# Cross attention's softmax tiles and context as fp16 pairs transposed by DMA, gate products on VectorE, in a decoder layer kernel

## The chip, the cores and the metric

One core of one Trainium2 chip runs the whole program. The metric is device time in microseconds (us); for a kernel on one core that is the time of this core. The kernel before took 362.12 us, the median of 3 runs (362.05 to 362.48).

## The reference

One decoder layer on x of 8 batches x 512 tokens x 256 features, in fp32, with a context of the same shape:

```python
x = x + _L0_attn_ref(_layernorm(x), head_dim_mask, w_q, w_k, w_v, w_o)
x = x + _L0_xattn_ref(_layernorm(x), ctx, mask, W, b)
x = x + _L0_ffn_ref(_layernorm(x), w_gate, w_up, w_down)

# _L0_attn_ref: q, k, v = x @ w_q, x @ w_k, x @ w_v        (256 -> 128)
#   y = (softmax(q k^T / sqrt(128)) v * head_dim_mask) @ w_o
# _L0_xattn_ref: x_proj = relu(x W^T + b); y_proj = relu(ctx W^T + b)   (256 -> 256)
#   scores = x_proj y_proj^T, -inf where the mask is set; y = softmax(scores) ctx
# _L0_ffn_ref: bitlinear(x, w) = _act_quant(x) @ _weight_quant(w)^T
#   gate = silu(bitlinear(x, w_gate)); up = bitlinear(x, w_up)          (256 -> 1024)
#   y = bitlinear(gate * up, w_down)                                    (1024 -> 256)
#   _act_quant: a row is scaled to 127 over its maximum and rounded
#   _weight_quant: mean of |w| is the scale, values rounded to -1, 0, 1
```

## The kernel before

A batch n (0 to 7) is one unit: 512 tokens, as T = 4 tiles of 128 tokens on the partitions, 256 features as DC = 2 chunks of 128. The work is written as steps of four streams: A is self attention, B cross attention, C the feed-forward part, E the projection of the context; W and F prepare weights, and S names the DMA transfers of a batch. Five lists written out by hand (PE_ORDER, ACT_ORDER, DVE_ORDER, POOL_ORDER and SP_ORDER, L102 to L250) give the order of the steps on TensorE (PE), ScalarE (ACT), VectorE (DVE), GpSimd (POOL) and on the DMA queue of SyncE (SP). Each engine runs its list in order, and every step waits on semaphores for its inputs and for the buffers that it overwrites. Three or four batches are in work at once: at a given time A is at batch n+3, B at n+2 and C at n or n+1.

fp32 precision comes from pairs: a value is split into a rounded high part and a rest, hi + lo, and a product is three matmuls, hi x hi, lo x hi and hi x lo (`product3`, L1133 to L1137, which all products by pairs share, so that their rows differ by tile names). The usual split of a result in PSUM is one ScalarE copy that rounds (hi) and one VectorE subtraction (lo).

Stream A: norms on VectorE and GpSimd (power of -0.5, L745), projections Q, K, V, four score steps S0 to S3, exponential on ScalarE (L931). For batches n > 0 the exponential of a tile goes to PSUM (the bank of its S step), ScalarE rounds it to fp16 (`p16`, L888) and VectorE subtracts for the rest (L1539); a DMA transposes the pair of the tile (`p16T`, L604), and the H step multiplies it by the fp16 pair of V.

Stream E, B: the transposed context (`ctxT_raw`) is loaded, rounded on ScalarE (`round_ctxT`) and its rest taken on GpSimd (`ctxT_rest`); W is split in the same way (`wt_hi`, `wt_lo`). YP0 and YP1 are the projection of the context, with relu (`yp_relu`) and a rest on GpSimd. XT0 and XT1 transpose the normed x on TensorE, their results are split (L941, L1594), XP0 and XP1 project. A tile t of cross attention then is: S_t, the scores (six matmuls of 512 columns: two chunks by three products); VectorE adds the mask and takes the maximum into `b_p` and `b_nmax` (L1600); ScalarE's exponential with the sum (L961); P_t, four TensorE transposes of `b_p` into a PSUM bank (L1280); ScalarE rounds them (`b_pT_hi`, L939), VectorE takes the rest (`b_pT_lo`, L1594); O_t, twelve matmuls of 256 columns by the context (`ctx_hi` from `round_ctx` on ScalarE, L975, and `ctx_lo` from `ctx_rest` on GpSimd, L689), and VectorE adds the result, scaled, to x (L1605). `b_p` and `b_pT` have two slots; the B steps alternate between the two banks b0 and b1.

Stream C: x is quantised (bf16), transposed by DMA (`xqT`), and for each tile pair j of 0 to 7 there is a gate product g_j and an up product u_j (L1352). ScalarE takes tanh of the gate (L1023); VectorE multiplies (t + 1) by g (L1624). For n < 6 ScalarE copies the up product out of PSUM (L1026) and GpSimd multiplies the two (`gated`, L753); for n = 6 and 7 VectorE multiplies them directly from PSUM (L1619). Then h is quantised over its row maximum (L1651, L800), copied to bf16 by ScalarE (L1033), transposed by DMA (`hT`, L612), and multiplied by the down weights (L1372).

## Time and profile before

| | value |
|---|---|
| device time, median of 3 runs | 362.12 us (362.05 to 362.48) |
| span of the profiled execution | 359.9 us |
| TensorE matmul busy | 349.1 us (97%) |
| TensorE weight load busy | 258.2 us (72%), beside matmuls |
| VectorE busy | 312.9 us (87%) |
| ScalarE busy | 313.7 us (87%) |
| GpSimd busy | 293.1 us (81%) |
| time of the packets of the DMA queue | 50.3% of 16 engines' span |

The span is one execution taken by the hardware profiler, from its first to its last instruction; 2.2 us lie between it and the median of the runs. Busy shares are means over a start of about 82 us without gate products and the rest with them. TensorE's instructions are pipelined, so the durations of neighbours overlap; the distance between their starts is what one costs. A row of the timeline gives start, duration, engine, line, operation, output <- input, shape and count; a group row gives busy time and mean ns of one, and then the idle time of the engine just before, with what ended most of it.

### The profile page before, as it was taken

What the parts mean: (1) busy time and instruction counts of PE and PEld (TensorE: products, weight loads), DVE (VectorE), ACT (ScalarE), POOL (GpSimd) and SP (SyncE); (2) the same over time, 40 slices, a digit from 0 to 9 for tenths busy, and PEclk for the clock granted to TensorE, in tenths of its full rate; (3) what the DMA queues carried; (4) which work ended last, traced back from release to release, by engine and by line L of the source; (5) the groups of instructions that cost most, each with busy time, mean ns of one, the idle gap of its engine ahead of it and who ended that gap; (6) DMA issues with size and microseconds to landing.
All of it is one profiled execution on the core that took longest, in us unless ns stands there. A gap on an engine that the chain in (4) does not pass through costs nothing.

```text
span 359.9 us, 7050 instructions
## 1 busy us (share of the span) xinstructions
PE 349.1 (97%) x1922; PEld 258.2 (72%) x1948; DVE 312.9 (87%) x916; ACT 313.7 (87%) x583; POOL 293.1 (81%) x421
## 2 busy tenths in 40 slices
PE   8999899999999999999999999999899999999996
PEld 6476578876887767776786678777587768667655
DVE  3769949948899899998899889999899889899994
ACT  2598999999899977999889986999679988987995
POOL 1657779369899998899968998899877997895886
PEclk9999999999999999999999999999999999999999
DMA  7986731725206644557275568238434633312353
GB/s 264 425 229 221 189 90 31 140 67 197 54 14 139 143 146 122 103 124 172 92 176 120 112 180 240 47 81 170 90 58 94 157 55 79 73 32 44 61 163 131
DMA packets 84695, 46.09 MB, mean 128 GB/s; under 512 B 76208, under 2 KB 77872, under 8 KB 84272
## 3 DMA queue, kind: packets, MB, share of 16 engines
q1 hardware_dynamic: 84656, 45.64, 50.3%
q8 instruction: 16, 0.26, 0.3%
q14 instruction: 23, 0.19, 0.2%
HBM read 23.07 MB, written 4.21 MB: 76 GB/s over the span
## 4 chain that ended last, share of the span: by engine, by line
PE 71%; DVE 8%; ACT 8%; POOL 5%; issue 5%; DMA 1%; SPq 1%; ACTq 0%; DVEq 0%; POOLq 0%
PE b_bank L1135 7%; PE b_bank L1136 7%; PE b_bank L1137 7%; PE d_bank L1372 5%; PE g_bank L1352 5%; PE a_bank L1135 5%; PE u_bank L1352 5%; PE a_bank L1137 5%; PE a_bank L1136 5%; PE b_bank L1280 2%; PE a_bank L1217 2%; POOL xp_lo L706 2%; PE b_bank L1251 1%; PE e_bank L1135 1%; PE e_bank L1137 1%
## 5 line engine op out<-in xcount | busy, mean ns | idle before, releaser
L753 POOL TENSOR_TENSOR c_work<-c_work 128x512 f32<-128x512 f32 x48 | 61.4, 1290 | 6.5 <-DVE c_work L1624 4.6
L1023 ACT ACTIVATE c_work<-g_bank,c_tanh_scale 128x512 f32<-128x512 f32 x52 | 36.1, 693 | 4.2 <-PE g_bank L1352 2.4
L1135 PE MATMUL b_bank<-ctx_hi,b_pT_hi 128*128 128x256 f32 x128 | 39.1, 306 | 0.2 <-DVE b_nmax L1600 0.2
L1624 DVE SCALAR_TENSOR_TENSOR c_work<-c_work,g_bank 128x512 f32<-128x512 f32 x50 | 33.9, 677 | 5.1 <-ACT c_work L1023 4.8
L1136 PE MATMUL b_bank<-ctx_lo,b_pT_hi 128*128 128x256 f32 x128 | 36.1, 282 | 0.0
L1137 PE MATMUL b_bank<-ctx_hi,b_pT_lo 128*128 128x256 f32 x128 | 36.1, 282 | 0.0
L800 POOL TENSOR_SCALAR c_work<-c_work,h_q 128x1024 f32<-128x1024 f32 x28 | 31.7, 1133 | 5.1 <-DVE h_q L1658 5.0
L1026 ACT ACTIVATE c_work<-u_bank 128x512 f32<-128x512 f32 x48 | 28.9, 602 | 5.4 <-PE u_bank L1352 5.0
L1352 PE MATMUL g_bank<-gateT,xqT 128*128 128x512 bf16 x98 | 30.5, 381 | 1.5 <-ACT xqT L998 0.5
L1352 PE MATMUL u_bank<-upT,xqT 128*128 128x512 bf16 x101 | 31.1, 381 | 0.8 <-DMA xqT<-xq 0.2
L1651 DVE TENSOR_REDUCE h_max<-c_work 128x1 f32<-128x1024 f32 x26 | 31.4, 1207 | 0.2 <-issue 0.2
L1372 PE MATMUL d_bank<-downT,c_half 128*128 128x256 bf16 x240 | 31.2, 273 | 0.0
L1372 PEld LDWEIGHTS d_bank<-downT,c_half 128*128 128x128 bf16 x240 | 22.1, 98 | 8.2 <-issue 3.7
L1135 PE MATMUL b_bank<-yp_hi,xp_hi 128*128 128x512 f32 x64 | 27.5, 429 | 0.2
L1033 ACT ACTIVATE c_half<-c_work 128x1024 bf16<-128x1024 f32 x26 | 27.4, 1063 | 0.0
L961 ACT ACTIVATE b_p<-b_p,b_nmax 128x512 f32<-128x512 f32 x32 | 23.2, 726 | 3.6 <-DVE b_nmax L1600 3.4
L1135 PEld LDWEIGHTS b_bank<-ctx_hi,b_pT_hi 128*128 128x128 f32 x128 | 24.3, 190 | 2.7 <-issue 0.9
L1137 PE MATMUL b_bank<-yp_hi,xp_lo 128*128 128x512 f32 x64 | 25.1, 393 | 0.0
L1136 PE MATMUL b_bank<-yp_lo,xp_hi 128*128 128x512 f32 x64 | 25.1, 392 | 0.0
L1136 PEld LDWEIGHTS b_bank<-ctx_lo,b_pT_hi 128*128 128x128 f32 x128 | 24.4, 190 | 0.4
L1600 DVE CUSTOM_DVE_ANT_0 b_p<-b_bank,mask_add 128x512 f32<-128x512 f32 x32 | 21.9, 684 | 3.1 <-PE b_bank L1137 3.0
L1137 PEld LDWEIGHTS b_bank<-ctx_hi,b_pT_lo 128*128 128x128 f32 x128 | 24.3, 190 | 0.0
(357 smaller groups left out, 1202.0 us busy)
## 6 DMA issues: line engine op xcount, KB each, us to landing
ctx_raw<-in_ctx SPq DMA_DIRECT2D x8, 512.0 KB, 5.0
x_all<-in_x SPq DMA_DIRECT2D x7, 512.0 KB, 4.0
a_xT_raw<-in_x_t SPq DMA_DIRECT2D x7, 512.0 KB, 4.4
ctxT_raw<-in_ctx_t SPq DMA_DIRECT2D x7, 512.0 KB, 4.5
out<-x_all SPq DMA_DIRECT2D x7, 512.0 KB, 2.9
r_bc<-r_rows SPq DMA_DIRECT2D x7, 256.0 KB, 3.6
c_work<-in_w_gate SPq DMA_DIRECT2D x1, 1024.0 KB, 9.7
c_work<-in_w_up SPq DMA_DIRECT2D x1, 1024.0 KB, 11.7
```

The costliest lines, as they stand in the source:

```text
L753: pool.tensor_tensor(h[:, t % 2, half * HALF:(half + 1) * HALF], th[:, j % 2, :], up[:, j % 2, :], ALU.mult).then_inc(hs, 1)
L800: pool.tensor_scalar(h_tile(t, n), h_tile(t, n), h_q[:, t:t + 1], ROUND if n < LAST else ROUND_F16, ALU.mult, ALU.add).then_inc(h_rounds, 1)
L1023: act.activation(gate_tile(j, n), gu_bank("g", j, n), ACT.Silu if (n, j) in SILU else ACT.Tanh, scale=c_tanh_scale[:, j // 2:j // 2 + 1]). ...
L1026: act.activation(up[:, j % 2, :], gu_bank("u", j, n), ACT.Copy).then_inc(ups, 1)
L1033: act.activation(h_q8[:, t % 2, :], h_tile(t, n), ACT.Copy, bias=-ROUND).then_inc(hqs, 1)
L1135: pe.matmul(dst, l_hi, r_hi, start=first, stop=False)
L1136: pe.matmul(dst, l_hi, r_lo, start=False, stop=False)
L1137: return pe.matmul(dst, l_lo, r_hi, start=False, stop=last)
L1352: mm = pe.matmul(dst, xqT[:, t * DC + c, :], w[:, c, cols], start=c == 0, stop=c == DC - 1)
L1372: mm = pe.matmul(dn_bank(t, n)[:, 0:D], h_T[:, t % 2, f, :], downT[:, f, :], start=f == 0, stop=f == FC - 1)
L1624: dve.scalar_tensor_tensor(gate_tile(j, n), gate_tile(j, n), 1.0, gu_bank("g", j, n), ALU.add, ALU.mult).then_inc(gates, 1)
L1651: dve.tensor_reduce(h_max[:, one], h_tile(t, n), AX.X, ALU.max, apply_absolute_value=True).then_inc(h_maxes, 1)
```

## The change

- Cross attention's softmax tiles. `b_p` has four slots. VectorE's maximum now scales by the batch's factor `s_scale` and a new small step N adds a constant to it, so that the exponential lies in fp16's range. ScalarE's exponential stays in SBUF, ScalarE rounds it to fp16 (`b_p16`), GpSimd takes the rest (`b_p_rest`), and a DMA transposes the pair (`transpose_b_p`). The P steps on TensorE, their roundings and rests are gone. O_t multiplies fp16 pairs.
- Context. Its rows are scaled by one power of the batch's norm: ScalarE squares with a sum (step sq), TensorE sums over the partitions by a matrix of ones (SS), VectorE bounds it (sx), GpSimd takes powers and factors (pow), ScalarE rounds to fp16 (hi), VectorE takes the rest (lo), into `c16` (three slots). O uses it as it is; for YP two DMA transposes (`cT0`, `cT1`) make `c16T`, in the place of the seven loads of the transposed context. W becomes an fp16 pair in the same manner, and so does the normed x (`b_T16`). `YP_SLOTS` goes from 3 to 2.
- Self attention, n > 0: the exponential stays in SBUF, and the fp16 rest moves from VectorE to GpSimd (`p_rest`).
- Feed-forward: all gate products are VectorE's from PSUM; the up product's copies on ScalarE and `gated` on GpSimd are gone. Four gate slots in place of two for every batch.
- Small VectorE operations on pairs of tiles are merged (shifts, scales, reciprocals of the sums: one for four tiles).
- All five order lists are new. In them the O steps of a batch stand behind its four S steps with steps of A, C and E between, the first gate product g0/0 comes behind B.S3/1, and SP_ORDER has bT0 to bT3 and cT0, cT1 of each batch among the transposes of `p16`, `xq` and `c_half`.

The core of the diff (the order lists and declarations are left out):

```diff
-B_STEPS = ["XT0", "XT1", "XP0", "XP1", "S0", "S1", "P0", "S2", "P1", "O0", "S3", "P2", "O1", "P3", "O2", "O3"]
+B_STEPS = ["XT0", "XT1", "XP0", "XP1", "S0", "S1", "S2", "S3", "O0", "O1", "O2", "O3"]
...
-B_LO = ["XT0", "XT1", "P0", "P1", "P2", "P3"]
+B_LO = ["XT0", "XT1"]
 NBL = len(B_LO)
 X_SLOTS = 4
 AP_SLOTS = 4
-YP_SLOTS = 3
+YP_SLOTS = 2
+C_SLOTS = 3
-DVE_GATED = [(6, j) for j in range(8)] + [(7, j) for j in range(8)]
...
+            def transpose_c(part, n):
+                sp.wait_ge(c_los if part else c_his, c_rank(n))
+                if n > 1:
+                    sp.wait_ge(c16T_loaded[part], 16 * (n - 1))
+                    sp.wait_ge(e_filled, DC * n)
+                sp.dma_start(c16T[:, part], c16[:, n % C_SLOTS, part, :], transpose=True).then_inc(c16T_loaded[part], 16)
+
+            def transpose_b_p(t, n):
+                sp.wait_ge(b_p_los, T * n + t + 1)
+                if n > 0:
+                    sp.wait_ge(b_p16_loaded[t], 16 * n)
+                    sp.wait_ge(b_filled, b_rank(f"O{t}", n - 1))
+                sp.dma_start(b_p16T[:, t], b_p16[:, t, :], transpose=True).then_inc(b_p16_loaded[t], 16)
...
-            def ctx_rest(n):
-                pool.wait_ge(ctx_his, n + 1)
-                pool.tensor_tensor(ctx_lo[:, :, :], ctx_raw[:, :, :], f32(ctx_hi[:, :, :]), ALU.subtract).then_inc(ctx_split, 1)
+            pool.wait_ge(consts_set, 9)
+
+            def p_rest(t, n):
+                pool.wait_ge(a_his, a_hi_rank(f"P{t}", n))
+                pool.tensor_tensor(p16[:, t, S:2 * S], a_p[:, (T * n + t) % AP_SLOTS, :], p16[:, t, 0:S], ALU.subtract).then_inc(a_p_los, 1)
+
+            def b_p_rest(t, n):
+                pool.wait_ge(b_p_his, T * n + t + 1)
+                pool.tensor_tensor(b_p16[:, t, S:2 * S], b_p[:, t, :], b_p16[:, t, 0:S], ALU.subtract).then_inc(b_p_los, 1)
+
+            def w_powers():
...
+            def c_powers_of(n):
+                pool.wait_ge(c_norms, c_rank(n))
+                pool.tensor_tensor(c_pow[:, n, :], c_x[:, n, :], powers[:, :], ALU.pow).then_inc(c_powers, 1)
+                if n > 0:
+                    pool.wait_ge(c_powers, c_rank(n))
+                    pool.wait_ge(W_scaled, 2)
+                    pool.tensor_scalar(y_bias[:, n, :], w_bias[:, :], c_pow[:, n, 0:1], 1.0, ALU.mult, ALU.mult)
+                    pool.tensor_scalar(s_scale[:, n:n + 1], c_pow[:, n, 1:2], s_factor[:, :], 1.0, ALU.mult, ALU.mult).then_inc(c_factors, 1)
...
-            def gated(j, n):
-                t, half = j // 2, j % 2
-                pool.wait_ge(*((tanhs if n == LAST else gates), 2 * T * n + j + 1))
-                pool.wait_ge(*u_copied(j, n))
-                if half == 0 and T * n + t - 1 > 0:
-                    pool.wait_ge(hqs, T * n + t - 1)
-                pool.tensor_tensor(h[:, t % 2, half * HALF:(half + 1) * HALF], th[:, j % 2, :], up[:, j % 2, :],
-                                   ALU.mult).then_inc(hs, 1)
...
-                act.activation(p if n == 0 else a_bank(f"P{t}", n)[:, :], p, ACT.Exp,
+                act.activation(p, p, ACT.Exp,
                                bias=a_nmax[:, t:t + 1], accum_out=a_sum[:, t:t + 1]).then_inc(a_exped, 1)
 
             def b_hi(step, n):
                 act.wait_ge(b_filled, b_rank(step, n))
-                src = b_bank[B_STEPS.index(step) % 2][:, :]
-                if step[0] == "P":
-                    act.activation(b_pT_hi[:, int(step[1]) % 2, :, :].rearrange("p k q -> p (k q)"), src, ACT.Copy).then_inc(b_his, 1)
-                else:
-                    act.activation(b_T_hi[:, int(step[-1]), :], src, ACT.Copy).then_inc(b_his, 1)
+                act.activation(b_T16[:, 0, int(step[-1]), :], b_bank[B_STEPS.index(step) % 2][:, :], ACT.Copy).then_inc(b_his, 1)
+
+            def b_p_hi(t, n):
+                act.wait_ge(b_exped, T * n + t + 1)
+                if n > 0:
+                    act.wait_ge(b_p16_loaded[t], 16 * n)
+                act.activation(b_p16[:, t, 0:S], b_p[:, t, :], ACT.Copy).then_inc(b_p_his, 1)
...
+            def square_ctx(n):
+                act.wait_ge(ctx_loaded, 16 * c_rank(n))
+                if n >= C_SLOTS:
+                    act.wait_ge(b_filled, b_rank("O3", n - C_SLOTS))
+                act.activation(c16[:, n % C_SLOTS, 0, :], ctx_raw[:, :, :].rearrange("p t d -> p (t d)"), ACT.Square,
+                               accum_out=c_ss[:, n:n + 1]).then_inc(c_squares, 1)
+
             def round_ctx(n):
-                act.wait_ge(ctx_loaded, 16 * n + 16)
-                if n > 0:
-                    act.wait_ge(ctx_split, n)
-                    act.wait_ge(b_filled, b_rank("O3", n - 1))
-                act.activation(ctx_hi[:, :, :], ctx_raw[:, :, :], ACT.Copy).then_inc(ctx_his, 1)
-
-            def round_ctxT(n):
-                act.wait_ge(ctxT_loaded, 16 * n)
-                if n > 1:
-                    act.wait_ge(ctxT_split, n - 1)
-                    act.wait_ge(e_filled, DC * n)
-                act.activation(ctxT_hi[:, :, :], ctxT_raw[:, :, :], ACT.Copy).then_inc(ctxT_his, 1)
...
-                else:
-                    act.wait_ge(u_filled, 2 * T * n + j + 1)
-                    act.activation(up[:, j % 2, :], gu_bank("u", j, n), ACT.Copy).then_inc(ups, 1)
...
-                    mm = product3(dst[:, :], wt_hi[:, k, c * P:(c + 1) * P], wt_lo[:, k, c * P:(c + 1) * P],
-                                  ctxT_hi[:, k, :], ctxT_lo[:, k, :], k == 0, k == DC - 1)
+                    mm = product3(dst[:, :], w16[:, 0, k, c * P:(c + 1) * P], w16[:, 1, k, c * P:(c + 1) * P],
+                                  c16T_chunks[:, 0, k], c16T_chunks[:, 1, k], k == 0, k == DC - 1)
...
-                elif step[0] == "P":
-                    pe.wait_ge(b_exped, T * n + t + 1)
-                    if t == 1:
-                        pe.wait_ge(b_los, b_lo_rank("P0", n))
-                    elif t == 2:
-                        pe.wait_ge(*o_read(0, n))
-                    elif t == 3:
-                        pe.wait_ge(b_los, b_lo_rank("P2", n))
+                else:
+                    pe.wait_ge(b_p16_loaded[t], 16 * n + 16)
+                    if t == 0:
+                        pe.wait_ge(c_los, c_rank(n))
+                    if t < 2:
+                        pe.wait_ge(b_maxed, T * n + t + 3)
+                    else:
+                        pe.wait_ge(*o_read(t - 2, n))
+                    hi, lo = (c16[:, n % C_SLOTS, part, :].rearrange("p (t d) -> p t d", t=T) for part in range(2))
                     for kc in range(T):
-                        mm = pe.transpose(dst[:, kc * P:(kc + 1) * P], b_p[:, t % 2, kc * P:(kc + 1) * P], ident[:, :])
-                else:
-                    pe.wait_ge(b_los, b_lo_rank(f"P{t}", n))
-                    if t == 0:
-                        pe.wait_ge(ctx_split, n + 1)
-                        pe.wait_ge(b_maxed, T * n + 3)
-                    elif t == 1:
-                        pe.wait_ge(b_maxed, T * n + 4)
-                    elif t == 2:
-                        pe.wait_ge(*o_read(1, n))
-                    for kc in range(T):
-                        mm = product3(dst[:, 0:D], b_pT_hi[:, t % 2, kc, :], b_pT_lo[:, t % 2, kc, :],
-                                      ctx_hi[:, kc, :], ctx_lo[:, kc, :], kc == 0, kc == T - 1)
+                        mm = product3(dst[:, 0:D], b_p16T[:, t, kc, :], b_p16T[:, t, T + kc, :], hi[:, kc, :], lo[:, kc, :], kc == 0, kc == T - 1)
                 mm.then_inc(b_filled, 1)
...
-                    elif step[0] == "P":
-                        t = int(step[1])
-                        last = dve.tensor_tensor(p16[:, t, S:2 * S], src[:, :], p16[:, t, 0:S], ALU.subtract)
...
-                        hi, lo = (z[:, t % 2, :, :].rearrange("p k q -> p (k q)") for z in (b_pT_hi, b_pT_lo))
-                    else:
-                        hi, lo = b_T_hi[:, t, :], b_T_lo[:, t, :]
-                    dve.tensor_tensor(lo, src[:, :], f32(hi), ALU.subtract).then_inc(b_los, 1)
+                    dve.tensor_tensor(b_T16[:, 1, t, :], src[:, :], b_T16[:, 0, t, :], ALU.subtract).then_inc(b_los, 1)
                 elif step[0] == "S":
                     if t == 0:
                         dve.wait_ge(masks_set, n + 1)
+                        if n == 0:
+                            dve.wait_ge(W_scaled, 2)
+                            dve.wait_ge(qkv_split, 1)
+                            dve.wait_ge(v_abs, 1)
                     dve.wait_ge(b_filled, b_rank(step, n))
-
-                    dve.tensor_tensor_reduce(b_p[:, t % 2, :], src[:, :], mask_add[:, :], -1.0, -MASKED, ALU.add, ALU.min,
-                                             b_nmax[:, t:t + 1]).then_inc(b_maxed, 1)
+                    if n > 0:
+                        dve.wait_ge(b_p_los, T * (n - 1) + t + 1)
+
+                    dve.tensor_tensor_reduce(b_p[:, t, :], src[:, :], mask_add[:, :], s_scale[:, n:n + 1], -MASKED, ALU.add, ALU.min,
+                                             b_min[:, t:t + 1]).then_inc(b_maxed, 1)
+                elif step[0] == "N":
+                    dve.wait_ge(b_maxed, T * n + t + 1)
+                    if n > 0:
+                        dve.wait_ge(b_exped, T * (n - 1) + t + 1)
+                    dve.tensor_scalar(b_nmax[:, t:t + 1], b_min[:, t:t + 1], P_TOP, None, ALU.add).then_inc(b_nmaxes, 1)
...
+            def split_ctx(n):
+                dve.wait_ge(c_his, c_rank(n))
+                hi, lo = c16[:, n % C_SLOTS, 0, :], c16[:, n % C_SLOTS, 1, :]
+                dve.scalar_tensor_tensor(lo, ctx_raw[:, :, :].rearrange("p t d -> p (t d)"), c_pow[:, n, 0:1], hi, ALU.mult, ALU.subtract).then_inc(c_los, 1)
...
+                    dve.wait_ge(b_exped, T * n + T)
+                    dve.wait_ge(c_powers, c_rank(n))
+                    if n > 0:
+                        dve.wait_ge(*o_added(T - 1, n - 1))
+                    dve.tensor_scalar(b_scaled_sum[:, :], b_sum[:, :], c_pow[:, n, 0:1], None, ALU.mult).then_inc(b_sums_scaled, 1)
+                    dve.wait_ge(b_sums_scaled, n + 1)
+                    dve.reciprocal(b_inv[:, :], b_scaled_sum[:, :]).then_inc(b_invs, 1)
```

## Rows read from the trace of the kernel before

**Rows 1.** The page: busy time by engine, and the DMA queue's share.

```profile
PE 349.1 (97%) x1922; PEld 258.2 (72%) x1948; DVE 312.9 (87%) x916; ACT 313.7 (87%) x583; POOL 293.1 (81%) x421
...
q1 hardware_dynamic: 84656, 45.64, 50.3%
```

**Rows 2.** Stretches: length, PE, PEld, DVE, ACT, POOL busy (count), clock, DMA.

```profile
30.00:82.00 52.00, 49.93 (x254) 38.99 (x255) 40.98 (x141) 48.83 (x90) 36.64 (x45) 1.00 0.50 118
82.00:357.00 275.00, 270.19 (x1561) 200.44 (x1584) 252.59 (x724) 246.47 (x461) 241.78 (x353) 1.00 0.47 110
```

**Rows 3.** Timeline of TensorE, at 82 us and from 165 to 175.

```profile
82.06 0.38 PE L1352 MATMUL g_bank<-gateT,xqT 128*128 128x512 bf16 x1
...
165.03 1.05 PE L1372 MATMUL d_bank<-downT,c_half 128*128 128x256 bf16 x8
165.91 0.38 PE L1352 MATMUL u_bank<-upT,xqT 128*128 128x512 bf16 x1
...
167.51 0.58 PE L1135 MATMUL b_bank<-yp_hi,xp_hi 128*128 128x512 f32 x1
167.93 0.39 PE L1136 MATMUL b_bank<-yp_lo,xp_hi 128*128 128x512 f32 x1
168.16 0.39 PE L1137 MATMUL b_bank<-yp_hi,xp_lo 128*128 128x512 f32 x1
...
172.10 0.38 PE L1136 MATMUL a_bank<-p16T,v16T 128*128 128x512 f16 x1
172.32 0.38 PE L1137 MATMUL a_bank<-p16T,v16T 128*128 128x512 f16 x1
172.53 0.60 PE L1280 MATMUL b_bank<-ident,b_p 128*128 128x128 f32 x4
172.97 0.59 PE L1352 MATMUL g_bank<-gateT,xqT 128*128 128x512 bf16 x2
173.33 0.36 PE L1135 MATMUL b_bank<-ctx_hi,b_pT_hi 128*128 128x256 f32 x1
...
174.83 0.40 PE L1135 MATMUL b_bank<-yp_hi,xp_hi 128*128 128x512 f32 x1
```

**Rows 4.** VectorE: two rows of its timeline, and one of its groups.

```profile
102.38 0.68 DVE L1547 TENSOR_TENSOR k_lo<-a_bank,k_hi 128x512 fp32r<-128x512 f32 x1
102.98 0.68 DVE L1541 TENSOR_TENSOR vT<-a_bank,vT 128x512 f16<-128x512 f32 x1
...
L1565 DVE TENSOR_SCALAR a_nmax<-a_max 128x1 f32<-128x1 f32 x32 | 4.7, 149 | 0.5
```

**Rows 5.** ScalarE: two rows of its timeline, and two of its groups.

```profile
97.01 0.60 ACT L939 ACTIVATE b_pT_hi<-b_bank 128x512 fp32r<-128x512 f32 x1
97.50 0.59 ACT L898 ACTIVATE k_hi<-a_bank 128x512 fp32r<-128x512 f32 x1
...
L961 ACT ACTIVATE b_p<-b_p,b_nmax 128x512 f32<-128x512 f32 x32 | 23.2, 726 | 3.6 <-DVE b_nmax L1600 3.4
L975 ACT ACTIVATE ctx_hi<-ctx_raw 128x1024 fp32r<-128x1024 f32 x8 | 8.6, 1074 | 0.0
```

**Rows 6.** GpSimd: groups of the page and of the lines.

```profile
L753 POOL TENSOR_TENSOR c_work<-c_work 128x512 f32<-128x512 f32 x48 | 61.4, 1290 | 6.5 <-DVE c_work L1624 4.6
...
L689 POOL TENSOR_TENSOR ctx_lo<-ctx_raw,ctx_hi 128x1024 fp32r<-128x1024 f32 x8 | 19.2, 2401 | 0.7 <-ACT ctx_hi L975 0.6
L745 POOL TENSOR_TENSOR b_rstd<-b_var,neg_half 128x2 f32<-128x2 f32 x16 | 11.2, 700 | 1.2
```

**Rows 7.** DMA issues, a stretch, and the SP queue's timeline and waits.

```profile
p16T<-p SPq DMA_TRANSPOSE x28, 2.8
...
96.00:99.00 3.00, 3.00 (x20) 2.61 (x19) 2.48 (x6) 3.00 (x8) 3.00 (x7) 1.00 0.48 93
...
96.07 1.23 SPq L612 DMA_TRANSPOSE c_half<-c_half  x1
...
SPq L612 <- ACT c_half L1033: 39.0, 15, 8.9
```

More of the change, by code:

```diff
@@ L45 @@
 E_BANK = "e"
+FIRST_SUM_BANK = "b0"
 def a_heir(step, n):
-    if n > 0 and step == "VT":
-        return "V"
-    return "S" + step[1] if n > 0 and step[0] == "P" else None
+    return "V" if n > 0 and step == "VT" else None
 def a_tables():
@@ L70, in a_tables @@
             else:
-                if step[:2] != "YP":
+                if step[:2] not in ("YP", "SS"):
                     place[step, n] = len(place)
-                banks[step, n] = E_BANK if part is later and step[:2] == "YP" else next(turn)
+                if step == "SS":
+                    banks[step, n] = FIRST_SUM_BANK if n < 2 else E_BANK
+                else:
+                    banks[step, n] = E_BANK if part is later and step[:2] == "YP" else next(turn)
                 before[step, n] = last.get(banks[step, n])
@@ L407, in decoder_layer @@
         qkv_hi, qkv_split = sem("qkv_hi"), sem("qkv_split")
+        W_squared, W_summed, W_normed, W_scaled = sem("W_squared"), sem("W_summed"), sem("W_normed"), sem("W_scaled")
         W_hi, W_split = sem("W_hi"), sem("W_split")
+        c_squares, c_sums, c_norms, c_powers, c_factors = (sem(f"c_{s}") for s in ("squares", "sums", "norms", "powers", "factors"))
+        c_his, c_los, c16T_loaded = sem("c_his"), sem("c_los"), [sem("c16T_hi_loaded"), sem("c16T_lo_loaded")]
         w_sums, dve_w_sums, w_totals = sem("w_sums"), sem("dve_w_sums"), sem("w_totals")
@@ L1463, in b_norm @@
                     dve.wait_ge(b_rstds, 2 * k)
-                    for t in pair(half):
-                        last = dve.tensor_scalar(b_shift[:, t:t + 1], b_mv[:, t, 0:1], b_rstd[:, t:t + 1], -1.0, ALU.mult, ALU.mult)
-                    last.then_inc(b_shifts, 1)
+                    two = slice(2 * half, 2 * half + 2)
+                    dve.scalar_tensor_tensor(b_shift[:, two], b_mv[:, two, 0], -1.0, b_rstd[:, two], ALU.mult, ALU.mult).then_inc(b_shifts, 1)
             def c_norm(part, i, n):
@@ L1483, in c_norm @@
                     dve.wait_ge(c_rstds, 2 * k)
-                    for t in pair(i):
-                        last = dve.tensor_scalar(c_shift[:, t:t + 1], c_mv[:, t, 0:1], c_rstd[:, t:t + 1], -1.0, ALU.mult, ALU.mult)
-                    last.then_inc(c_shifts, 1)
+                    two = slice(2 * i, 2 * i + 2)
+                    dve.scalar_tensor_tensor(c_shift[:, two], c_mv[:, two, 0], -1.0, c_rstd[:, two], ALU.mult, ALU.mult).then_inc(c_shifts, 1)
             def last_aggr(t):
@@ L1514, in scale_x @@
                         dve.wait_ge(c_scales, k - 2)
-                    for t in pair(half):
-                        last = dve.tensor_scalar(c_s[:, t:t + 1], c_amax[:, t:t + 1], AMAX_MIN, 1.0 / Q_MAX, ALU.max, ALU.mult)
-                    last.then_inc(xq_steps, 1)
+                    dve.tensor_scalar(c_s[:, two], c_amax[:, two], AMAX_MIN, 1.0 / Q_MAX, ALU.max, ALU.mult).then_inc(xq_steps, 1)
                 else:
```

533 lines of the change are left out of this document (285 added, 248 removed).

## The prediction

> **What bounds the kernel now.** I read the page's busy line first: TensorE 97%, VectorE and ScalarE 87% each, GpSimd 81% [rows 1]. Busy shares of matmuls can flatter, so the second view was TensorE's timeline. Starts follow each other without a hole: fp32 pair products of 512 columns every 0.23 us (167.93 to 168.16), 16-bit ones of 512 columns every 0.215 (172.10 to 172.32 to 172.53), and the twelve matmuls of a context product take 1.50 us from 173.33 to 174.83 [rows 3]. The reader should see there that durations (0.38, 0.28) overlap and that only the distance of starts is a cost. The third view is busy time by stage [rows 2]. The first gate matmul starts at 82.06 us [rows 3]. Until then ScalarE has 48.8 us in 52; from there to 357 TensorE has 270.2 us in 275 (98%), while VectorE has 252.6, ScalarE 246.5 and GpSimd 241.8. So two stages with two bounds: ScalarE (with TensorE) before the gates, TensorE after. The span is 359.9 us; the median of the runs is 362.12, 2.2 more, which I add at the end.
>
> A rule stands against trusting the 97%. The Trainium skill (Perfetto Trace Analysis, Identifying the Most-Contended Engine) says that matmul busy time is no good measure of how close a kernel is to the roofline, and that the busy share of weight loads is one. By that the reader would put TensorE at 258 us of 360 and see no bound in it. The trace's starts without holes disagree for this kernel, and the matter comes back as a rival.
>
> **The change on TensorE.** Removed: the transposes of the cross-attention softmax tiles, 32 steps of four matmuls; one takes 0.44 us (172.53 to 172.97) [rows 3]: 14.1 us. The 32 context products go from fp32 pairs to fp16 pairs. Nearest row: the down product, eight 16-bit matmuls of 256 columns in 0.88 us (165.03 to 165.91), 0.11 each, so twelve take 1.32 for 1.50 [rows 3]: 32 x 0.18 = 5.8 us. The projections of x (96 matmuls) and of the context (84) go to 16-bit too: 180 x (0.23 - 0.215) = 2.7 us. An fp32 product right behind a 16-bit one has a slow first matmul, 0.42 us to the next start (167.51 to 167.93) where the following take 0.23 [rows 3]; of the 30 projection steps I count half as having this, 15 x 0.19 = 2.9 us. Added: nine one-column sums over ones, at 0.2 to 0.25 us each, 2 us (no row of before has this form; between 0.1 and 0.4 each it is 1 to 4). Sum: 14.1 + 5.8 + 2.7 + 2.9 - 2 = 23.5, 24 us less, 349 to 325.
>
> **VectorE.** Its durations overlap as well: 0.68 us for a 128x512 operation on PSUM, but 0.60 from start to start (102.38 to 102.98) [rows 4]. Removed: the fp16 rests of 28 self-attention tiles and the rests of 32 cross-attention tiles, 60 x 0.60 = 36.0 us. Added: 48 gate products from PSUM at 0.60, 28.8 us; 8 context rests of 1024 elements at twice 0.60, 9.6; 32 small sums for the exponent's bias at 0.08 to 0.15 (the row of the same operation in self attention [rows 4]), 3.8; 9 small norms, 1.4. Merged: reciprocals 32 to 8 with a scale before each, -2; 44 small pair operations saved at 0.1, -4.4. Sum: +1. In the stage after the first gate it is nil too: by the new order 48 products come in there, and 48 rests (20 + 28) go; the small ones cancel. VectorE keeps 252.6 us there.
>
> **ScalarE.** Removed: 48 copies of the up product out of PSUM, start to start 0.49 (97.01 to 97.50; duration 0.60) [rows 5]: 23.2 us, and 7 roundings of the transposed context at 0.95: 6.7. Added: 8 squares of the context, the duration of the context's rounding, 1.07, with its accumulator [rows 5]: 8.8; the weight's 0.7; 60 roundings that now read SBUF instead of PSUM, 0.05 each by my estimate, 3. Sum: 17 less, 314 to 297. But four squares and four roundings lie before the first gate, where ScalarE is the tight engine: with two exponentials that moved up it gets some 5 us more there.
>
> **GpSimd.** Removed: 48 gate products at 1.27 to 1.29, 61.4 us busy; the context rests, 8 x 2.4, and their transposed twins, 7 x 2.4: 36 [rows 6]. Added: 60 rests at the same form's 1.27, 76 us; powers and factors, 8 x (0.7 for a power like b_rstd's, + 2 x 0.23) and 1.6 once: 11. Sum: 10 less, 293 to 283. That an fp16 output and input keep the price is unknown: a 16-bit-writing scalar operation suggests no more, twice would be the upper end. The engine has 60 us of slack, so up to 0.9 us more on each tile stays hidden.
>
> **Queues.** Transposes by DMA rise by 46 (32 softmax tiles, 14 context halves) from 77. One holds the SP queue 1.23 us, lands after 2.8 us and takes 0.48 x 3 = 1.44 us of all 16 DMA engines [rows 7]. So 66 us more DMA work, about 15 less for the 7 loads that go, on some 181 us now (50.3% of 359.9 [rows 1]): two thirds of the span, no bound by share. SP gets 57 us more of issuing. Here a page speaks against the change. The Trainium skill (VectorE: DVE Perf Modes, The three transpose paths) gives 1309 ns for a 128x128 tile by DMA against 390 ns on TensorE; by its figure eight blocks would be an estimated 10.5 us per tile and the DMA the bound. The trace has 2.8 us for a tile of eight blocks, so it disagrees for this shape.
>
> The softmax path of a tile becomes: maximum 0.68 (as other operations of its size on PSUM [rows 4]), bias 0.15, exponential 0.73 and rounding 0.6 [rows 5], rest 1.29, transpose 2.8: 6.3 us, some 7.5 with the hops between engines. In the new order TensorE has, between the end of the first score step and the first context product, by my count at the distances of [rows 3] 9.8 us of other steps in batch 0, 8.8 in the last and 11 to 17 in between. So it is covered, if the tile's transpose is not queued behind a waiting one.
>
> **The sum.** Front: ScalarE's 5 us more at 94% would put the first gate at 87; its remaining holes can take some, so I take 85 (82 to 89). From there TensorE has 270 less 21 and less the 3 us net of steps that the order moves before the gates: 246. ScalarE has 246.5 less the 23 of the copies, 224; GpSimd 241.8 less 61 and nine context rests (22) plus 48 rests (62) and the powers, 223 to 227; VectorE 252.6. VectorE is next. TensorE alone was packed to 98%; with a second engine within 3% of it I take 97%: 260 us. 85 + 260 + 2.9 (last addition to the end) = 348, and 2.2 to the runs: 350 us.
>
> **The rivals.** (a) VectorE takes over as above: 345 to 356, 350; chance 0.50. (b) TensorE stays the bound and all of its 24 us show: 362.1 - 24 = 338; for it speaks that VectorE's total (314) is below TensorE's (325) and that a new order can use VectorE's 11 idle us before the gates; against it the stage count; 0.20. (c) The gain is lost between the two: gates begin at 88, VectorE is packed to 94% (269): 360 to the end, 362. This is also where the page's rule leads: if TensorE were no bound, its saving would buy nothing, and 361 to 362 would stay; 0.15, of which a third within 0.2%. (d) Slower: SP's queue is in order, and it waits long for a quantised h tile already (39.0 us in total, 8.9 the longest [rows 7]). A softmax tile's transpose stands behind such a wait; then the context product waits, and on TensorE all steps behind it. The cover in a batch is 2 to 9 us, so the rival decides from delays of about 5 us per batch: eight stalls of 3 us eat the 24, at 3.6 us it is 367. For it speaks the number of transposes, against it that SP idles often; 0.12. (e) GpSimd's fp16 rests cost twice, 76 us more, and it becomes the bound at about 370; 0.03.
>
> **How the numbers follow.** The likeliest is (a), 350. The range: (b) down to 339, (c) up to 361; outside lie half of (b) and the slower cases. Something like 0.2% is what a measurement tells from no change. Faster: (a), (b) and most of (c), 0.82; within 0.2%: 0.05; slower: 0.13.
>
> **What would show it.** After: TensorE near 325 us busy, the tile transposes' rows gone, context products at 0.11 us from start to start; VectorE's busy time within 3 us of before and its share near 91%; gates near 85 us; the idle time before VectorE's groups down from 22 us after the gates to about 8, before TensorE's up. Wrong if TensorE waits for the transposed softmax tiles for more than some us in total, if GpSimd's rests are above 1.5 us, or if ScalarE's front pushes the first gate past 90 us.

## The result: 364.45 us after 362.48 us, a loss of 0.55% where 3% were forecast to be gained

The changed kernel takes 364.45 us, the median of 9 runs (361.79 to 365.35); the kernel before, in 9 runs, 362.48 (361.59 to 363.14). The ratio is 1.0055, with a 95% interval of 1.0033 to 1.0076. The forecast was 350, and 361 the upper end of the range. The profiled execution of after has a span of 361.3 us, where before has 359.9.

The page of after, busy time by engine and the DMA queue's share (of before: [rows 1]):

```profile
span 361.3 us, 6967 instructions
PE 336.1 (93%) x1813; PEld 218.8 (61%) x1838; DVE 327.9 (91%) x893; ACT 298.0 (82%) x546; POOL 282.5 (78%) x447
...
q1 hardware_dynamic: 132224, 54.04, 68.4%
```

ScalarE lost 15.7 us (forecast: 17), GpSimd 10.6 (10), the DMA share is 68% ("two thirds"). TensorE lost 13 of busy time. VectorE gained 15.0 us, where the forecast had 1.

The same two stretches of after as in [rows 2], and a row from 93 us on, as the first gate product of after starts at 92.97:

```profile
30.00:82.00 52.00, 46.67 (x223) 29.49 (x222) 38.88 (x124) 47.05 (x88) 38.99 (x44) 0.97 0.79 178
82.00:357.00 275.00, 261.23 (x1479) 171.26 (x1502) 268.87 (x718) 232.30 (x424) 229.08 (x372) 1.00 0.67 137
...
93.00:357.00 264.00, 250.94 (x1435) 164.45 (x1459) 258.85 (x694) 223.88 (x410) 218.70 (x354) 1.00 0.69 140
```

VectorE is busy 268.87 of 275 us, 98%. It has taken TensorE's place in [rows 2] (270.19). Where its 15 us come from is seen in its groups. Those of the small operations and of the new large ones, after:

```profile
L1640 DVE CUSTOM_DVE_ANT_0 b_p<-b_bank,mask_add,s_scale 128x512 f32<-128x512 f32 x32 | 23.7, 743 | 4.3 <-PE b_bank L1180 4.0
L1783 DVE SCALAR_TENSOR_TENSOR c<-ctx_raw,c_pow,c 128x1024 f16<-128x1024 f32 x8 | 12.7, 1581 | 0.3 <-ACT c L1024 0.3
L1529 DVE SCALAR_TENSOR_TENSOR c_shift<-c_mv,c_rstd 128x2 f32<-128x2 f32 x14 | 6.3, 449 | 0.7 <-POOL c_rstd L783 0.7
L1815 DVE TENSOR_SCALAR b_scaled_sum<-b_sum,c_pow 128x4 f32<-128x4 f32 x8 | 5.6, 698 | 0.0
L1558 DVE TENSOR_SCALAR c_s<-c_amax 128x2 f32<-128x2 f32 x14 | 5.1, 363 | 0.1
L1510 DVE SCALAR_TENSOR_TENSOR b_shift<-b_mv,b_rstd 128x2 f32<-128x2 f32 x16 | 4.0, 251 | 0.1
L1817 DVE RECIPROCAL b_inv<-b_scaled_sum 128x4 f32<-128x4 f32 x8 | 1.4, 178 | 0.3
```

And the same work before, in operations of one element:

```profile
L1465 DVE TENSOR_SCALAR b_shift<-b_mv,b_rstd 128x1 f32<-128x1 f32 x32 | 5.1, 202 | 0.0
L1485 DVE TENSOR_SCALAR c_shift<-c_mv,c_rstd 128x1 f32<-128x1 f32 x28 | 4.5, 203 | 2.3 <-POOL c_rstd L745 2.3
L1755 DVE RECIPROCAL b_inv<-b_sum 128x1 f32<-128x1 f32 x32 | 4.2, 150 | 0.1
L1516 DVE TENSOR_SCALAR c_s<-c_amax 128x1 f32<-128x1 f32 x28 | 2.9, 147 | 0.2
```

120 operations of one element took 16.7 us. The 60 that stand in their place take 22.4; eight of them, the products `b_scaled_sum`, are new. A product of four numbers in each partition takes 0.7 us in the mean. Its single executions show why. Three rows of VectorE's timeline of after, and then the rows of GpSimd's timeline beside them:

```profile
138.54 1.08 DVE L1815 TENSOR_SCALAR b_scaled_sum<-b_sum,c_pow 128x4 f32<-128x4 f32 x1
...
259.66 1.09 DVE L1815 TENSOR_SCALAR b_scaled_sum<-b_sum,c_pow 128x4 f32<-128x4 f32 x1
...
327.84 1.13 DVE L1815 TENSOR_SCALAR b_scaled_sum<-b_sum,c_pow 128x4 f32<-128x4 f32 x1
```

```profile
138.44 1.16 POOL L709 TENSOR_TENSOR b_p<-b_p 128x512 f16<-128x512 f32 x1
...
259.56 1.16 POOL L709 TENSOR_TENSOR b_p<-b_p 128x512 f16<-128x512 f32 x1
...
326.67 2.27 POOL L709 TENSOR_TENSOR b_p<-b_p 128x512 f16<-128x512 f32 x2
```

Each ends 0.02 to 0.03 us behind GpSimd's instruction: 139.62 behind 139.60, 260.75 behind 260.72, 328.97 behind 328.94. The shortest execution of the same operation takes 0.20 us. VectorE stands inside its own instruction until GpSimd's ends, and the trace books that as busy. Counted one by one, as what an execution takes above the shortest of its row, this is 12.8 us in four merged groups (`c_shift` 4.3, `b_scaled_sum` 4.0, `c_s` 2.8, `b_shift` 1.7), and each of the 20 executions prolonged by over 0.1 us ends 0.00 to 0.03 us behind a GpSimd instruction. (The expectations of experiments 1 and 9 were written on a first, lower count and have 10.7 and 12.9.) The context's rests, which read two tiles from SBUF, add 2.4: three of the eight are long, and these end 1.07 to 1.08 us behind a GpSimd instruction, so they look held up until it had ended. Together 15.2 us. In the trace of before the same count gives nothing.

Size alone is not what makes an operation wait. Reciprocals of two and four elements never did, in before or after:

```profile
L1561 DVE RECIPROCAL c_q<-c_s 128x2 f32<-128x2 f32 x14 | 2.2, 157 | 0.1
L1809 DVE RECIPROCAL a_inv<-a_sum 128x4 f32<-128x4 f32 x8 | 1.3, 167 | 0.0
```

The Trainium skill (SBUF — State Buffer, Who interferes with whom) states this: VectorE and GpSimd share a pair of SBUF ports as an exclusive lock, which a VectorE instruction needs if it has two SBUF inputs or runs in a two-port mode, and whoever has it keeps it for the whole instruction. The rows agree: the product above took 1.08 us beside a GpSimd instruction of 1.16. It is the page that the prediction should have weighed.

### The profile page after: what moved, and what is told of

It reads as the page before. It is cut to its first block, busy times and chain, and to the rows that moved or that the text cites. A ratio compares the mean times of both kernels' runs of the same rounds, so it can differ in the third digit from the quotient of the medians.

```text
span 361.3 us, 6967 instructions
## 1 busy us (share of the span) xinstructions
PE 336.1 (93%) x1813; PEld 218.8 (61%) x1838; DVE 327.9 (91%) x893; ACT 298.0 (82%) x546; POOL 282.5 (78%) x447
## 4 chain that ended last, share of the span: by engine, by line
DVE 29%; PE 28%; issue 14%; DMA 11%; POOL 9%; ACT 6%; SPq 2%; DVEq 0%; POOLq 0%; ACTq 0%
PE b_bank L1178 4%; PE b_bank L1179 4%; PE b_bank L1180 4%; PE d_bank L1411 3%; DVE c_work L1669 3%; DMA b_p16T<-b_p 3%; DVE c_work L1664 3%; PE g_bank L1391 2%; POOL xp_lo L741 2%; DMA c16T<-c 2%; PE u_bank L1391 2%; DVE h_max L1696 2%; DVE a_bn L1476 2%; DVE b_T L1628 2%; PE a_bank L1178 2%
## 5 line engine op out<-in xcount | busy, mean ns | idle before, releaser
L709 POOL TENSOR_TENSOR b_p<-b_p 128x512 f16<-128x512 f32 x32 | 37.8, 1191 | 1.9 <-ACT b_p L973 1.7
L705 POOL TENSOR_TENSOR p<-a_p,p 128x512 f16<-128x512 f32 x28 | 32.4, 1164 | 7.0 <-ACT p L918 7.0
L1178 PE MATMUL b_bank<-c,b_p16T 128*128 128x256 f16 x128 | 35.0, 273 | 2.7 <-DMA b_p16T<-b_p 2.7
L1664 DVE TENSOR_TENSOR c_work<-c_work,u_bank 128x512 f32<-128x512 f32 x52 | 35.2, 678 | 0.5 <-ACT c_half L1073 0.2
L1179 PE MATMUL b_bank<-c,b_p16T 128*128 128x256 f16 x128 | 34.9, 273 | 0.0
L1180 PE MATMUL b_bank<-c,b_p16T 128*128 128x256 f16 x128 | 34.9, 273 | 0.0
L1178 PE MATMUL b_bank<-yp_hi,xp_hi 128*128 128x512 f32 x64 | 28.4, 443 | 0.8 <-DVE b_min L1640 0.6
L1411 PEld LDWEIGHTS d_bank<-downT,c_half 128*128 128x128 bf16 x240 | 22.4, 98 | 9.4 <-issue 3.5
L1640 DVE CUSTOM_DVE_ANT_0 b_p<-b_bank,mask_add,s_scale 128x512 f32<-128x512 f32 x32 | 23.7, 743 | 4.3 <-PE b_bank L1180 4.0
L1180 PE MATMUL b_bank<-yp_hi,xp_lo 128*128 128x512 f32 x64 | 25.2, 393 | 0.0
L741 POOL TENSOR_TENSOR xp_lo<-b_relu,xp_hi 128x512 fp32r<-128x512 f32 x16 | 20.9, 1317 | 4.9 <-ACT xp_hi L992 4.9
L736 POOL TENSOR_TENSOR yp_lo<-e_relu,yp_hi 128x512 fp32r<-128x512 f32 x16 | 20.5, 1279 | 4.9 <-ACT yp_hi L987 4.9
```

What stands on the lines that cost most here:

```text
L705: pool.tensor_tensor(p16[:, t, S:2 * S], a_p[:, (T * n + t) % AP_SLOTS, :], p16[:, t, 0:S], ALU.subtract).then_inc(a_p_los, 1)
L709: pool.tensor_tensor(b_p16[:, t, S:2 * S], b_p[:, t, :], b_p16[:, t, 0:S], ALU.subtract).then_inc(b_p_los, 1)
L1178: pe.matmul(dst, l_hi, r_hi, start=first, stop=False)
L1179: pe.matmul(dst, l_hi, r_lo, start=False, stop=False)
L1180: return pe.matmul(dst, l_lo, r_hi, start=False, stop=last)
L1411: mm = pe.matmul(dn_bank(t, n)[:, 0:D], h_T[:, t % 2, f, :], downT[:, f, :], start=f == 0, stop=f == FC - 1)
```

## The experiments

The theory to be tested, V: VectorE is the bound of the changed kernel, and the waits for the port put it there. The rivals: T, the transposes by DMA and the late start set the time; P, TensorE still does; G, the time that passes until GpSimd's results are there sets it. Times of different experiments are compared by their ratios to the kernel before, which was run beside each.

**1. The merges undone.** In the changed kernel:

```diff
-                    dve.scalar_tensor_tensor(c_shift[:, two], c_mv[:, two, 0], -1.0, c_rstd[:, two], ALU.mult, ALU.mult).then_inc(c_shifts, 1)
+                    for t in pair(i):
+                        last = dve.tensor_scalar(c_shift[:, t:t + 1], c_mv[:, t, 0:1], c_rstd[:, t:t + 1], -1.0, ALU.mult, ALU.mult)
+                    last.then_inc(c_shifts, 1)
```

and `b_shift`, `c_s` and `b_scaled_sum` in the same way.

> The changed kernel with its four merged small VectorE operations (the two shifts, the scale of x, the product of the four sums with the context's factor) as operations of one element each again, as before; nothing else changes. In the profile after, VectorE is busy 97.8% from 82 to 357 us, and 10.7 us of these operations' time are waits that end with a GpSimd instruction. Theory V (VectorE is the bound, and the port it shares with GpSimd holds it): busy time of VectorE falls from 327.9 to about 318, no row of these lines above 0.3 us, and the time falls by most of it, to 353 to 356 us. Rival T (the transposes by DMA and the late start set the time, VectorE's share is high because it waits inside its instructions for nothing in particular): VectorE's busy time falls but the time stays within 1 us of 364.

Measured: 360.42 us, ratio to the kernel before 0.9925 (0.9898 to 0.9953), and a second time (run for comparison with experiment 10):

> The first experiment once more, beside the last one on the same chip: ratio to the kernel before 0.990 to 0.995 as the first time.

359.94 us, ratio 0.9933 (0.9904 to 0.9962). The page of the first:

```profile
span 358.7 us, 7035 instructions
PE 335.3 (93%) x1813; PEld 219.2 (61%) x1838; DVE 322.3 (90%) x961; ACT 297.7 (83%) x546; POOL 282.5 (79%) x447
```

And one of its groups of VectorE, which answers to L1815 above:

```profile
L1820 DVE TENSOR_SCALAR b_scaled_sum<-b_sum,c_pow 128x1 f32<-128x1 f32 x32 | 4.5, 202 | 0.0
```

68 instructions more, and the kernel is 1.3% faster than the changed one, and 0.7% faster than the kernel before. The one-by-one count of waits falls from 15.2 to 1.0 us, and what is left stands in the context's rests. Theory V's direction holds and T's does not. But the size is off: by the ratios the time fell by 4.7 us (4.4 the second time), not by 8 to 11. VectorE's busy time fell by 5.6 and not by 10: 14.2 us of waits went, and the 68 instructions more brought 8.6 back.

**2. The merges alone, in the kernel before** (both shifts and `c_s` of two elements).

> The kernel before with three of the merges alone (both shifts and the scale of x as operations of two elements): 44 instructions fewer on VectorE. Theory V: these rows go from 0.1 to 0.16 us for one element to 0.3 to 0.5 us on the mean for two, with single ones above 1 us beside GpSimd's instructions; VectorE's busy time rises by 2 to 6 us in place of falling by 4. As TensorE bounds that kernel, the time rises by 0 to 2 us only. Rival (the merges cost nothing there): rows of 0.15 us, busy time 4 us less, time unchanged.

VectorE's groups of these lines in that kernel:

```profile
L1513 DVE TENSOR_SCALAR c_s<-c_amax 128x2 f32<-128x2 f32 x14 | 6.9, 495 | 0.2
L1484 DVE SCALAR_TENSOR_TENSOR c_shift<-c_mv,c_rstd 128x2 f32<-128x2 f32 x14 | 6.1, 437 | 2.2 <-POOL c_rstd L745 2.2
L1465 DVE SCALAR_TENSOR_TENSOR b_shift<-b_mv,b_rstd 128x2 f32<-128x2 f32 x16 | 3.7, 235 | 0.0
```

VectorE 316.7 us busy in place of 312.9, with 44 instructions fewer; time 363.00, ratio 1.0009 (0.9985 to 1.0033). The count of waits is 10.4 us. As theory V expected: the price of the merge on VectorE is there without the rest of the change, and where VectorE has room, no loss of time shows within the interval.

**3. Half the bytes of the new transposes.**

```diff
-                sp.dma_start(b_p16T[:, t], b_p16[:, t, :], transpose=True).then_inc(b_p16_loaded[t], 16)
+                sp.dma_start(b_p16T[:, t, 0:T], b_p16[:, t, 0:S], transpose=True).then_inc(b_p16_loaded[t], 16)
```

> The changed kernel, in which the transposes of cross attention's softmax tiles move the high halves alone (half the bytes of 32 transposes), and the context product takes them for the rests too. Theory V: DMA share falls by some 6 points from 68.4%, the time by less than 1 us. Rival T: TensorE's waits for these tiles and for other transposes behind them on SP's queue shrink, and the time falls by 3 us or more.

Measured: 364.76 us, ratio 1.0053 (1.0023 to 1.0082), DMA share 61.3%. (The product takes the high halves in the place of the rests too.) The median from issue to landing went from 3.7 to 3.0 us. The same time as the changed kernel's 1.0055, within the intervals. Rival T falls in its part on the bytes of these transposes; their number, and what each holds of SP's queue, was not changed.

**4. Less work on VectorE than that.** Experiment 1, with the gate products of batches 0 to 5 on `HALF // 2` columns.

> The first experiment, and besides the 48 gate products of batches 0 to 5 on half their columns (half of h is not computed): takes another 48 x 0.28 = 13 us off VectorE. Theory V: with VectorE down to some 304 us TensorE (251 us from the first gate to 357) is next, and the time falls by another 3 to 7 us, to 347 to 351. Rival T: no further change, below 1 us.

Measured: 357.00 us, ratio 0.9841 (0.9798 to 0.9884); VectorE 311.0 us busy. Half of h is not computed in these batches. Another 11.3 us off VectorE gave 3 us (0.0084 of 362, from four runs; 1.2 to 4.9 by the two intervals). The fall is at the lower end of V's 3 to 7; the 347 to 351 expected for the time was missed, as experiment 1's had been. VectorE's work still counts, at 0.3 us for each us, where experiment 1 gave 0.8 (4.7 for 5.6). In the stretch 93 to 354 us VectorE is at 93% there, TensorE at 95%.

**5 and 6. The same 14 us off TensorE, before and after.** The context product without its third matmul:

```diff
-                        mm = product3(dst[:, 0:D], b_p16T[:, t, kc, :], b_p16T[:, t, T + kc, :], hi[:, kc, :], lo[:, kc, :], kc == 0, kc == T - 1)
+                        mm = product2(dst[:, 0:D], b_p16T[:, t, kc, :], b_p16T[:, t, T + kc, :], hi[:, kc, :], lo[:, kc, :], kc == 0, kc == T - 1)
```

> The kernel before, whose context product leaves out one of its three products (high context by the tile's rests): 128 matmuls of 256 columns fewer, by the distance of starts 0.12 us each, 15 us off TensorE. If TensorE bounds that kernel, as the prediction said, its time falls by 8 us or more (VectorE is then next). Rival (both engines' shares are only high, neither bounds alone): 3 us or less.

> The changed kernel with the same product left out, 128 x 0.11 = 14 us off TensorE. Theory V (VectorE bounds the changed kernel): the time falls by less than 1.5 us, TensorE's idle time takes the rest. Rival P (TensorE still bounds it, its 336 us of busy time are real): it falls by 5 us or more.

In the kernel before: 356.97 us, ratio 0.9840 (0.9815 to 0.9865), 5.8 us less. In the changed kernel: 362.80, ratio 1.0016 (0.9989 to 1.0043), which is 1.4 us less than the changed kernel's 1.0055. This pair shows that TensorE's part in the time has shrunk: 15 us of its work were worth 5.8 us before (less than the 8 expected; that VectorE close behind took the rest is argued, not shown), 14 are worth 1.4 after (0.2 to 2.7 by the two intervals). It also bears on the rule that was weighed in the prediction, that of the Trainium skill (Perfetto Trace Analysis, Identifying the Most-Contended Engine). By its measure, the share of weight loads, the prediction saw no bound in TensorE at 72% [rows 1]; in the run TensorE's work did set part of the time.

**7. Relief for VectorE through GpSimd.** Experiment 1, with the shifts computed on GpSimd behind the power.

> The first experiment, with the 60 one-element shifts of cross attention's and the feed-forward's norms computed on GpSimd right behind the power that they need, in place of VectorE: 9.7 us busy off VectorE (7.2 by distance of starts), some 16 us more on GpSimd (60 x 0.27), and no way back through VectorE's list for the norms. Theory V: the time falls by 2 to 4 us from the first experiment's, to 356 to 358. Rival G (GpSimd's latency for the rests and powers sets the time as much): no gain or a loss, 360 to 364.

Measured: 361.79 us, ratio 0.9994 (0.9965 to 1.0022): slower than experiment 1 by 0.7% although VectorE has 4.9 us less to do (317.4). Theory V's 356 to 358 is missed, and the time is rival G's (360 to 364). GpSimd has 15.7 us more to do (298.2).

**8. One gate product in eight back on ScalarE and GpSimd.** Experiment 1, and for j = 7, n < 6 a copy out of PSUM (`C.u7`) and a product on GpSimd in place of VectorE's `C.M7`.

> The first experiment, with the last of the eight gate products of each batch 0 to 5 given back as it was before the change: ScalarE copies the up product out of PSUM, GpSimd multiplies. 6 x 0.6 = 3.6 us off VectorE, 2.9 us more on ScalarE, 7.6 on GpSimd. Theory V: 0.5 to 2 us faster than the first experiment. Rival G: slower than it, as GpSimd's product takes twice as long and lies between the gate and the maximum over h.

Measured: 383.24 us, ratio 1.0586 (1.0553 to 1.0620). VectorE's waits, first row (waited for: us in total, times, longest):

```profile
DVE h_max L1633 <- POOL c_work L705: 22.2, 6, 4.5
```

Theory V's gain is missed again, and rival G's loss is there, 6.7% over experiment 1. The maximum over h stood in VectorE's list where VectorE's own product had been ready; with GpSimd's it waits 3.7 us in the mean, six times, and its list is in order. It says nothing against the old division of the work as such, whose lists were made for it; it shows what a wait costs on an engine that has little idle time.

**9. GpSimd's operations in halves**, VectorE's program untouched:

```diff
+                for k in range(0, S, S // 2):
+                    last = pool.tensor_tensor(b_p16[:, t, S + k:S + k + S // 2], b_p[:, t, k:k + S // 2], b_p16[:, t, k:k + S // 2], ALU.subtract)
+                last.then_inc(b_p_los, 1)
```

> The changed kernel, VectorE's program untouched; GpSimd's rests of the softmax tiles and of both projections and its scaling of h are issued as two operations of half the columns. If the 12.9 us in VectorE's merged operations are waits for a GpSimd instruction to end, they halve, to 5 to 8 us, and VectorE's busy time falls from 327.9 to 321 to 323, while GpSimd's rises by some 120 x 0.05 to 0.1 us. Theory V: time 1 to 4 us less than the changed kernel's 364. Rival (those rows are long for a reason of their own, their form): unchanged rows, time same or worse.

Measured: 365.94 us, ratio 1.0096 (1.0061 to 1.0131); the waits of the four merged groups are 12.8 us by the one-by-one count, as without the edit, not 5 to 8. (With the context's rests 14.1.) VectorE is busy 326.8 us, GpSimd 303.9, 21 more, where 6 to 12 were expected; so this edit was not the pure one that was meant. A row of VectorE, and then GpSimd's of the same time:

```profile
139.59 2.65 DVE L1825 TENSOR_SCALAR b_scaled_sum<-b_sum,c_pow 128x4 f32<-128x4 f32 x1
```

```profile
139.54 1.41 POOL L741 TENSOR_TENSOR yp_lo<-e_relu,yp_hi 128x256 fp32r<-128x256 f32 x2
140.91 1.30 POOL L712 TENSOR_TENSOR b_p<-b_p 128x256 f16<-128x256 f32 x2
```

My expectation was wrong in its mechanism. VectorE's instruction ends at 142.24, behind four GpSimd operations (142.21): it did not get in between them. Shorter operations did not shorten this wait, as they followed each other without a hole. The rival, that the form is slow by itself, falls too: the end is again GpSimd's end.

**10. Additions moved off VectorE that only the store needs.** Experiment 1, with `POOL_DN` taking in tiles 1 and 3 of batches 0 to 3.

> The first experiment, with eight of the additions of the down product to x (tiles 1 and 3 of batches 0 to 3) moved from VectorE to ScalarE (scaled copy out of PSUM) and GpSimd (addition), as the last batches have it; nothing but the store waits for them. 8 x 0.4 = 3.1 us off VectorE by distance of starts, 4 on ScalarE, 6 on GpSimd. Theory V: 0.5 to 1.5 us faster than the first experiment. Rival G: no gain, the added work in GpSimd's list delays the rests behind it.

Measured: 395.63 us, ratio 1.0891 (1.0839 to 1.0942), where theory V expected a gain. SP's waits (L541 is the store of a batch), and then TensorE's first row:

```profile
SPq L541 <- POOL x_all L751: 37.0, 5, 11.9
```

```profile
PE b_bank L1086 <- DMA b_p16T<-b_p: 16.2, 3, 11.0
```

"Nothing but the store waits for them" was wrong. The store stands in SP's list ahead of the transposes, and GpSimd's addition stands later in its list than VectorE's did; so SP waits up to 11.9 us with the softmax tiles' transposes behind it, and TensorE 11.0 us for one of them. This is the prediction's rival (d), made by another edit: it exists, and the change as it was timed does not trigger it.

**12. The factor of the sums on ScalarE.** Experiment 1 with

```diff
+            def scale_sums(n):
+                act.wait_ge(b_exped, T * n + T)
+                act.wait_ge(c_powers, c_rank(n))
+                act.activation(b_scaled_sum[:, :], b_sum[:, :], ACT.Copy, scale=c_pow[:, n, 0:1]).then_inc(b_sums_scaled, 1)
```

> The first experiment, in which the four sums of a batch are multiplied by the context's factor on ScalarE (one operation of 128x4 behind the last rounding of the batch) in place of four on VectorE: 32 small operations, 4.5 us busy, off VectorE, 8 x 0.2 to 0.3 us on ScalarE, GpSimd untouched. Theory V: 1 to 3 us faster than the first experiment (359.9 to 360.4), at 357 to 359, VectorE near 317 us busy. Rival (with the port waits gone VectorE no longer bounds, as moving work to GpSimd suggested): no change from the first experiment.

Measured: 363.38 us, ratio 1.0022 (1.0002 to 1.0041): 1% slower than experiment 1, with 5.0 us less of work on VectorE (317.3). VectorE's waits, first row:

```profile
DVE b_inv L1825 <- ACT b_scaled_sum L1004: 7.3, 6, 2.6
```

4.5 us of work were exchanged for 7.3 us of waiting in VectorE's list. Theory V's gain of 1 to 3 us is missed. Neither side of the expectation had this: the rival's "no change" is nearer, but not for its reason.

**What the experiments leave of theory V.** Shown: the waits inside the merged operations (rows), that undoing them gives 4.4 to 4.7 us (experiments 1 and 11), that less work on VectorE gives some more (4), and that TensorE's work gives little now (6). Not shown: that VectorE's busy time alone sets the rest. The four edits that gave work of VectorE to other engines (7, 8, 10, 12) all made the kernel slower than experiment 1, each by waits or delays of its own. When VectorE's inputs arrive counts beside how much it has to do, as rival G has it.

## Why the prediction was wrong

**The step that failed is VectorE's sum.** The forecast was made from VectorE: 314 us of work and, in a span of 348, 34 us without. In the trace of after VectorE is busy 327.9 us and idle 33.4 (361.3 - 327.9). The idle part was right within 1 us, which is luck in part, as the stages below show; the work was 14 short, and the span is 13.3 longer than forecast. Within the sum it was the term "merged: -2 and -4.4". Rows show 22.4 us in place of 16.7, +5.7 for -6.4, so it is off by 12.1 us. The context's rests were 12.7 for 9.6, as they wait for the port too, and the maximum with a scale from memory takes 743 ns for 684 (L1640), 1.9 us. The three are 17 us. Three operations of the start that read two tiles from SBUF take 3.2 us more than before, which no term covered (1.75, 2.02 and 1.85 us for 0.69, 0.95 and 0.82). That these exceed the 14 lies in the way of counting: the terms were made with distances of starts, and stand here against durations. I priced the merge as instructions saved at 0.1 us each. The rows of before with two and four elements are reciprocals (0.16 and 0.17 us), another form than the merged ones, and no row showed the merged forms beside a busy GpSimd: I should have bounded it from both sides, and the upper end was a GpSimd operation (1.29 us [rows 6]) for each.

How much of the miss does that term explain in time? Undoing it gave back 4.4 to 4.7 us of 14, and that turns the loss against the kernel before into a gain of 0.7%. What the waits alone cost, with the merges and no waits, was not tried. By the account of busy and idle time the rest of the distance to 350 is the other side of the same term (the saving of 6.4 us did not exist with single operations either: they take 18.5 us for the 16.7 of before, and VectorE is busy 322.3 us for the 314 forecast) and 2.4 us more idle time (358.7 - 322.3 = 36.4). This is an account and no experiment: experiments 7 and 12 brought VectorE to 317 us busy, and the time did not follow. What sets these last 10 us stays open.

**The first gate product: forecast 85, measured 92.97 us.** Wrong by 8, and past the 90 us that the prediction had named as a sign of being wrong. In its own sum (85 + 260 + 2.9) the front is 8.0 us of the 13.3, and the stretch from the first gate to the last addition 5.3 (92.97 to 358.30). The merges are not what delays it: in experiment 1 the first gate is at 92.58. Nor is it ScalarE's load, by which it was priced: ScalarE is busy 73.61 of the first 93 us (79%). Cross attention's last addition of batch 0 starts at 76.3 us for 73.7 before, so up to there the front is 2.6 us late, about the 3 that I gave it. Part of the rest is order: more of other work stands ahead of the gates than the 3 us I counted (VectorE has 68.5 us busy in 0 to 93, 59.85 in 0 to 82 before), and it is missing behind them: without the waits VectorE has some 246 us from 93 to 357, where 252.6 were forecast from 85. Part is idle time: TensorE has 9.1 us of it in 0 to 93, 3.1 in 0 to 82 before. That the errors of front and stage largely cancel is argued. Whether an earlier gate would help was not tried.

**TensorE: forecast 24 us less.** The tile transposes are gone and a context product of after runs at 0.11 us from start to start (108.06 to 109.26 us are eleven such distances), as worked out. Its busy time fell by 13 only. Some 3.5 us of the difference are the way of counting: a matmul before an idle time counts with its whole length, and the holes of the timeline rose from 45 to 68. Summed by distances of starts (a matmul before a hole at the median of its form) TensorE's work went from 341.0 to 324.5 us, so 16.5 less where 24 were forecast. The context products gave 6.9 for the 5.8, the tile transposes 12.2 for 14.1; the projections gave 1.5 for 5.6, with 1.7 us of it lost at the lower clock (below). TensorE's idle time, the span less the busy time, rose from 10.8 to 25.2 us. The forecast that it would no longer be the bound fits experiment 6.

**ScalarE, GpSimd, DMA:** right within 2 us or 2 points. GpSimd's fp16 rests take 1.16 to 1.19 us, not more than the fp32 ones: rival (e) did not happen. The transposes of the softmax tiles land after 3.7 us (median of 32) where 2.8 was taken; TensorE's matmuls wait 2.7 us for them in all (its weight loads 5.0). The cover held, and rival (d) did not happen in this kernel.

**Rivals.** The time came out nearest to (c)'s, 362, but not by its mechanism: VectorE was to be packed to 94%, and it is at 98%, with more work. (b) was wrong, and the likeliest, (a), named the right bound at the wrong size. That the result is on the slower side was given 0.13, for two mechanisms that did not act; (d) and (e) as listed are 0.15 together, and the range, up to 361, leaves out (c)'s own 362. VectorE's share came out at the 91% that the prediction names, by luck: its busy time was to stay within 3 us and rose by 15.

## What to carry to other kernels

Before merging small VectorE operations, look at GpSimd's busy share and at the form: with one element in each partition `tensor_scalar` did not wait for GpSimd here, with two and four it did, and so did `scalar_tensor_tensor` with two SBUF inputs; reciprocals of two and four elements did not. The wait could last to the end of a whole run of GpSimd instructions (2.65 us in experiment 9). When a busy engine runs its list in order, price its waits as work: 7.3 us of waiting cost more than 4.5 us of work taken off it. And price an edit at an in-order DMA queue by what stands behind it: the store that "nothing waits for" cost 35 us (experiment 10 against 1).

The best version measured is experiment 1, at 0.9925 and 0.9933 of the kernel before.
